# Writing the one-hots of a graph kernel's two gather stages on GpSimd, with an eight-part row ring in the first

## The reference

```python
q, k, v = h @ Wq + bq, h @ Wk + bk, h @ Wv + bv     # layer 2, per node; 8 heads of 16
e = edge_attr @ We                                  # per edge
alpha = sum(q[dst] * (k[src] + e)) / 4              # per edge and head
a = exp(alpha - segment_max(alpha, dst)[dst])
out = segment_sum(a / segment_sum(a, dst)[dst] * (v[src] + e), dst)
...
x_src, x_dst, x_edge = ...                          # layer 4, per edge, of h[src] and h[dst]
gates = softmax(concat(x_src, x_dst, x_edge) @ W_gate + b_gate)
out = segment_sum(gates[0] * x_src + gates[1] * x_dst + gates[2] * x_edge, dst)
```

## Time and profile before

| | |
|---|---|
| median of 3 runs | 7088.67 us (7060.04 to 7090.18) |
| span of the profiled execution | 7080.9 us |
| keys-and-values stage, first gather to last score | 2370.6 to 3815.0, 1444.4 us |
| gate stage, first gather to last addition | 5607.2 to 7030.2, 1423.0 us |
| DVE work in one-hots, gate stage | 144.3 us (208 of 694 ns) |

### The profile page before, as it was taken

One profiled execution on the slowest core, in us unless ns is written; L12 is line 12 of the kernel. 1 busy time (PEld: TensorE's weight loads), 2 busy tenths in 40 slices (PEclk: granted clock), 3 DMA queues, 4 the chain that ended last, 5 costly groups with the idle time before them and its releaser, 6 DMA issues.

```text
span 7080.9 us, 98147 instructions
## 1 busy us (share of the span) xinstructions
PE 4162.5 (59%) x25513; PEld 3308.9 (47%) x25514; DVE 2977.6 (42%) x8318; ACT 1295.5 (18%) x3253; POOL 2894.8 (41%) x2784
## 2 busy tenths in 40 slices
PE   1112000599898455555563664798899666666664
PEld 1001000366565455555553563465565666556654
DVE  3438201411313344444446677212312555555556
ACT  0001000000100211111111664200200322322222
POOL 6778777000000265555553565000000255555555
PEclk6555555799899777777776996899999755655555
DMA  9713000366463455555552451464364222222222
GB/s 361 267 61 135 6 0 0 103 198 192 141 195 118 111 160 158 154 150 156 155 162 89 125 148 30 137 197 138 131 196 145 64 78 78 78 78 79 79 78 69
DMA packets 447985, 885.48 MB, mean 125 GB/s; under 512 B 91722, under 2 KB 278572, under 8 KB 441502
## 3 DMA queue, kind: packets, MB, share of 16 engines
q1 hardware_dynamic: 333406, 608.36, 27.1%
q0 software_dynamic: 106912, 224.30, 11.9%
q10 hardware_dynamic: 7584, 51.91, 2.0%
HBM read 728.93 MB, written 155.35 MB: 125 GB/s over the span
## 4 chain that ended last, share of the span: by engine, by line
PE 33%; DVE 20%; issue 19%; another core or an unknown queue 15%; DVEq 6%; DMA 2%; ACT 2%; ACTq 1%; SPq 0%; POOL 0%; POOLq 0%
PE ps L836 23%; DVE work L1603 3%; PE ps L992 2%; DVE work L624 2%; PE ps L415 1%; DVE work L368 1%; DMA hw<-d_keys 1%; DVE work L1202 1%; DVEq L342 1%; PE ps L1184 1%; DVE hw L438 1%; PE ps L843 1%; PE ps L1182 1%; DMA work<-attr_dram 1%
## 5 line engine op out<-in xcount | busy, mean ns | idle before, releaser
L361 POOL DMA_INDIRECT work<-tab_kv,src_col x832 | 814.1, 978 | 1758.7 <-DMA tab_kv<-hw 1142.1
L361 POOL DMA_INDIRECT work<-tab_gate,src_col x832 | 795.5, 956 | 1795.5 <-DMA tab_gate<-logits 1183.3
L484 POOL DMA_INDIRECT d_adj<-logits,address x782 | 848.1, 1085 | 276.6 <-issue 238.8
L836 PE MATMUL ps<-hw 128*128 128x384 bf16 x5096 | 863.4, 330 | 50.4 <-DVE hw L815 37.1
L836 PE MATMUL ps<-hw,work 128*128 128x384 bf16 x5096 | 845.1, 326 | 0.0
L415 PE MATMUL ps<-work 128*128 128x136 f32 (+1 forms) x3328 | 655.0, 360 | 131.6 <-DVE acc L438 86.4
L836 PEld LDWEIGHTS ps<-hw 128*128 128x128 bf16 x5096 | 502.1, 99 | 383.1 <-issue 53.7
L415 PEld LDWEIGHTS ps<-work 128*128 128x128 f32 x3328 | 599.8, 265 | 165.4 <-issue 165.4
L875 DVE TENSOR_TENSOR work<-work,ps 128x128 f32 (+1 forms) x208 | 59.9, 288 | 1410.0 <-ACT work L867 1409.2
L836 PEld LDWEIGHTS ps<-hw,work 128*128 128x128 bf16 x5096 | 498.8, 98 | 317.7
L1168 PE MATMUL ps<-ident,work 128*128 128x128 f32 x832 | 177.1, 350 | 656.8 <-ACT work L1158 285.2
(11 more groups left out here) (389 smaller groups left out, 6581.4 us busy)
## 6 DMA issues: line engine op xcount, KB each, us to landing
hw<-d_adj SPq DMA_DIRECT2D x104, 800.0 KB, 4.3
work<-d_adj SPq DMA_DIRECT2D x104, 800.0 KB, 4.4
d_adj<-acc SPq DMA_DIRECT2D x52, 1568.0 KB
hw<-d_adj SPq DMA_DIRECT2D x104, 768.0 KB, 4.2
work<-d_adj SPq DMA_DIRECT2D x104, 768.0 KB, 4.3
work<-attr_dram SPq DMA_DIRECT2D x832, 64.0 KB
d_value<-work SPq DMA_DIRECT2D x208, 256.0 KB
work<-d_value SPq DMA_DIRECT2D x208, 256.0 KB, 2.7
```

Of the source, the lines that this page charges most:

```text
L361: pool.indirect_dma_start(rows[:, r * U + u, 0:width], None, table, bass.IndirectOffsetOnAxis(sources[:, at:at + 1], 0)).then_inc(rows_in[ ...
L484: pool.indirect_dma_start(d_adj, bass.IndirectOffsetOnAxis(address[:, tile:tile + 1], 0), counts[:, tile:tile + 1], None).then_inc(adj_out ...
L836: last = nc.tensor.matmul(at, adj_half[2 * s + hf][:, k, :], xs[:, b, :], start=b == 0, stop=b == BLOCKS - 1)
```

## The change

The one-hots of the two gather stages are written by POOL: behind each gather it puts one 128x128 compare (`tensor_scalar`) for the same step. In the keys-and-values stage the ring of gathered rows gets eight parts: four in `rows`, four in the space of `acc`. Since `acc` is in use until the scores are done, the load of `resets` moves behind the last score on SP. Some semaphores are merged (`x_and_h`, `relu_ready`, `x_biased`, and three of the beta step), and `edge_loop` takes the number of parts.

```diff
-        def gathers(pool, k, table, width, sources, free):
+        def gathers(pool, k, table, width, sources, free, hot_free):
             for n in range(GATHER_TURNS[k] * PARTS):
                 r = n % PARTS
                 if n >= PARTS:
                     free(n - PARTS)
                 for u in range(U):
                     at = n * U + u
                     pool.indirect_dma_start(rows[:, r * U + u, 0:width], None, table,
                                             bass.IndirectOffsetOnAxis(sources[:, at:at + 1], 0)).then_inc(rows_in[r], 16)
+                    if u == 0 and n >= PARTS:
+                        hot_free(n - PARTS)
+                    ins = pool.tensor_scalar(hot[:, r * U + u, :], iota[:], rel_col[:, at:at + 1], None, ALU.is_equal)
+                ins.then_inc(sem("hot_ready"), 1)
...
+        def kv_rows(r):
+            return (near_rows if r < PARTS else far_rows)[:, r % PARTS * U:(r % PARTS + 1) * U, :]
         def att_pool(pool):
             pool.wait_ge(sem("table_out"), KV_TABLE)
-            gathers(pool, ATT_PASS, tab_kv, KV, src_col, lambda n: pool.wait_ge(sem("kv_done"), n + 1))
+            for n in range(ALL_PARTS):
+                r = n % FAR
+                if n >= FAR:
+                    pool.wait_ge(sem("kv_done"), n - FAR + 1)
+                for u in range(U):
+                    at = n * U + u
+                    pool.indirect_dma_start(kv_rows(r)[:, u, :], None, tab_kv,
+                                            bass.IndirectOffsetOnAxis(src_col[:, at:at + 1], 0)).then_inc(far_in[r], 16)
+                    if u == 0 and n >= PARTS:
+                        pool.wait_ge(sem("att_turned"), n - PARTS + 1)
+                    ins = pool.tensor_scalar(hot[:, n % PARTS * U + u, :], iota[:], rel_col[:, at:at + 1], None, ALU.is_equal)
+                ins.then_inc(sem("hot_ready"), 1)
...
-            edge_loop(dve, [(0, step_hot()), (2, scores)])
+            edge_loop(dve, [(2, scores)], FAR_TURNS, FAR)
...
-            gathers(pool, GATE_PASS, tab_gate, GATE_ROW, src_col, lambda n: pool.wait_ge(sem("gate_msg"), n + 1))
+            gathers(pool, GATE_PASS, tab_gate, GATE_ROW, src_col, lambda n: pool.wait_ge(sem("gate_msg"), n + 1),
+                    lambda n: pool.wait_ge(sem("win_done"), gate_sums.done0 + U * (n + 1)))
...
-            edge_loop(dve, [(2, logits), (3, message), (2, gates), (0, step_hot(hot_free)), (4, gate_sums.step_add(dve))])
+            edge_loop(dve, [(2, logits), (3, message), (2, gates), (4, gate_sums.step_add(dve))])
...
-            max_sp(sp)
             att_sp(sp)
+            sp.wait_ge(sem("kv_done"), ALL_PARTS)
+            max_sp(sp)
             sums_sp(sp)
```

More of the change, by code:

```diff
@@ L23 @@
 ALL_PARTS = TURNS * PARTS
+FAR = 8
+FAR_TURNS = ALL_PARTS // FAR
+assert FAR_TURNS * FAR == ALL_PARTS and FAR == 2 * PARTS
 PAIRS = -(-TILES // 2)
@@ L80, in wait, with edge_loop @@
         engine.wait_ge(sem, value)
-def edge_loop(engine, stages, turns=TURNS):
-    for r in range(PARTS):
+def edge_loop(engine, stages, turns=TURNS, parts=PARTS):
+    for r in range(parts):
         for lag, step in stages:
             if r >= lag:
-                step((r - lag) // PARTS, (r - lag) % PARTS)
+                step((r - lag) // parts, (r - lag) % parts)
     with engine.Fori(1, turns) as i:
-        for r in range(PARTS):
+        for r in range(parts):
             for lag, step in stages:
-                back = (r - lag) // PARTS
-                step(i + back if back else i, (r - lag) % PARTS)
+                back = (r - lag) // parts
+                step(i + back if back else i, (r - lag) % parts)
     for late in range(max(lag for lag, _ in stages)):
@@ L97, in edge_loop @@
             if late < lag:
-                step(turns + (late - lag) // PARTS, (late - lag) % PARTS)
+                step(turns + (late - lag) // parts, (late - lag) % parts)
 def pair_loop(engine, count, step):
@@ L223, in program @@
         rows = part(rows_flat, 0, (TURN, GATE_ROW))
+        near_rows, far_rows = part(rows_flat, 0, (TURN, KV)), part(acc_flat, 0, (TURN, KV))
         hot = part(hot_flat, 0, (TURN, P))
@@ L323, in program @@
         rows_in = [sem(f"rows_in{r}") for r in range(PARTS)]
+        far_in = rows_in + [sem(f"far_in{r}") for r in range(FAR - PARTS)]
         attr_in = [sem(f"attr_in{r}") for r in range(PARTS)]
@@ L345, in registers @@
             return values
[L350 removed]
+        GATHER_TURNS = (FAR_TURNS, TURNS)
         TURN0 = [sum(GATHER_TURNS[:k]) for k in range(len(GATHER_TURNS))]
[L353 removed]
+        def gathers(pool, k, table, width, sources, free, hot_free):
             for n in range(GATHER_TURNS[k] * PARTS):
@@ L1190, in scores @@
             def scores(i, r):
-                n = i * PARTS + r
+                n = i * FAR + r
                 e = banks(2 + 2 * (r % RING2)).rearrange("p (u f) -> p u f", u=U)
                 q = banks(3 + 2 * (r % RING2)).rearrange("p (u f) -> p u f", u=U)
-                key = rows[:, r * U:(r + 1) * U, 0:D]
+                key, its_value = kv_rows(r)[:, :, 0:D], kv_rows(r)[:, :, D:KV]
                 values = value[:, r % RING2 * U:(r % RING2 + 1) * U, :]
                 dve.wait_ge(sem("eq_done"), n + 1)
-                dve.wait_ge(rows_in[r], 16 * U * (ATT_TURN0 + i + 1))
-                wait(dve, value_out[r % RING2], 16 * (i * (PARTS // RING2) + r // RING2))
+                dve.wait_ge(far_in[r], 16 * U * (i + 1))
+                wait(dve, value_out[r % RING2], 16 * (i * (FAR // RING2) + r // RING2))
                 nc.vector.tensor_tensor(key, e, key, ALU.add).then_inc(sem("key_step"), 1)
-                nc.vector.tensor_tensor(values, e, rows[:, r * U:(r + 1) * U, D:KV], ALU.add)
+                nc.vector.tensor_tensor(values, e, its_value, ALU.add)
                 dve.wait_ge(sem("key_step"), 2 * n + 1)
@@ L1430, in beta_act @@
         def beta_act(act):
-            act.wait_ge(sem("beta_in"), 1)
+            act.wait_ge(sem("beta_dve"), 1)
             nc.scalar.activation(stat[:, 1, :], stat[:, 0, :], ACT.Exp, scale=-1.0).then_inc(sem("beta_exp"), 1)
@@ L1467, in att_end_dve @@
             chain.after(nc.vector.reciprocal(stat[:, 2, :], stat[:, 1, :]))
-            dve.sem_inc(sem("beta_ready"), 1)
+            dve.sem_inc(sem("beta_dve"), 1)
             with chain.loop(GROUPS, 1) as g:
@@ L1507, in mix_act @@
         def mix_act(act):
-            act.wait_ge(sem("beta_ready"), 1)
+            act.wait_ge(sem("beta_dve"), 2)
             with act.Fori(0, GROUPS) as g:
@@ L1747, in _ @@
             sp.wait_ge(sem("reset_out"), 16)
+            att_sp(sp)
+            sp.wait_ge(sem("kv_done"), ALL_PARTS)
             max_sp(sp)
-            att_sp(sp)
             sums_sp(sp)
@@ L2030, in kv_ready @@
                 dve.sem_inc(sem("kv_ready"), 1)
-                nc.vector.tensor_tensor(group(x, g), group(x, g), group(h, g), ALU.add).then_inc(sem("x_and_h"), 1)
+                nc.vector.tensor_tensor(group(x, g), group(x, g), group(h, g), ALU.add).then_inc(sem("x_added"), 1)
             p_qkv.dve(dve, behind=kv_ready)
-            dve.wait_ge(sem("x_and_h"), GROUPS)
+            dve.wait_ge(sem("x_added"), GROUPS)
             att_dve(dve)
@@ L2054, in relu @@
             def relu(g):
-                nc.vector.tensor_scalar(group(t, g), group(t, g), 0.0, None, ALU.max).then_inc(sem("relu_ready"), 1)
+                nc.vector.tensor_scalar(group(t, g), group(t, g), 0.0, None, ALU.max).then_inc(sem("x_added"), 1)
             p_sage1.dve(dve, behind=relu)
-            dve.wait_ge(sem("relu_ready"), GROUPS)
+            dve.wait_ge(sem("x_added"), 2 * GROUPS)
             dve.sem_inc(sem("self2_ready"), GROUPS)
@@ L2060, in _ @@
             p_self2.dve(dve, behind=lambda g: nc.vector.tensor_tensor(
-                group(x, g), group(x, g), bias("L2_bn2", GROUP), ALU.add).then_inc(sem("x_biased"), 1))
-            dve.wait_ge(sem("x_biased"), GROUPS)
+                group(x, g), group(x, g), bias("L2_bn2", GROUP), ALU.add).then_inc(sem("x_added"), 1))
+            dve.wait_ge(sem("x_added"), 3 * GROUPS)
             dve.sem_inc(sem("dense_open"), 1)
```

9 lines of the change are left out of this document (2 added, 7 removed).

## The result

The changed kernel takes 7857.56 us (median of 4 runs, 7800.25 to 7863.54) against 7089.43 us (7060.04 to 7124.37): a ratio of 1.1055, 95% interval 1.1007 to 1.1103. I had forecast 7235 us, and a range up to 7560. The direction was right, the size was not.

The account below looks back on a forecast made before the run. No engine was over 59% busy; POOL's waits, read as PE's counts arriving late behind close gathers, bounded the two stages. 7080.9 - 146 + 46 + 247 = 7228 us profiled, 7235 us median; range 6990 to 7560 us.

Parts of the forecast that it names:

- The compare's price: Both gather stages: each POOL compare adds 0.30 us to the 1.25 us gather pitch, taken from an affine select.
- a pitch nearer 1.9 us: Sign of a wrong prediction: POOL's step of gather and compare near 1.9 us instead of the forecast 1.55 us.
- 1664 c - 352 us: Whole kernel: the change's total effect, with c the cost of one POOL compare; nothing at c = 0.21.
- Rival 3: Both stages: compare costs 0.5 to 0.6 us because POOL switches between descriptors and elements; 7570 to 7735 us; chance 0.10.
- Keys-and-values stage: POOL sets the pace at 6.20 us a part, start hole of 45 us gone: 1298 us against 1444, -146 us.
- The resets: End of keys-and-values stage: the load moved behind the last score takes 48 us and delays the first scan; +46 us.
- Gate stage: POOL and PE wait for each other once a part: 7.98 us a part against 6.79, +247 us.
- The circle: Gate stage: POOL's last compare, PE's turn and sums, then POOL's next one-hot; 3.03 us, POOL standing 1.8 us a part.
- rival 4: POOL's compares and DVE's messages with two SBUF operands hold each other up: +115 us, 7350 us; chance 0.08.
- rival 2: Keys-and-values stage: PE's counts still arrive late while gathers follow each other, and POOL waits: 7565 us; chance 0.13.
- Rival 5: Gate stage: PE's clock rises to 2.4 GHz, shortening the mutual wait to 6.4 us a part: 6935 us; chance 0.03.
- Rivals 1 and 6: Compare mostly fits the gap between gathers, 6903 us at 0.1 us, chance 0.20; or costs near 0.21 us, terms cancel, 0.06.

Follow-up runs that it names:

- spaced: Kernel before plus a useless one-element POOL compare behind the first three gathers of each part, both stages: 6239.74 us against 5916.44, ratio 1.055.
- const_compare: Changed kernel with POOL comparing with a constant, not the targets' column, and one 128x512 compare a part in the gate stage: 6727.0 us in one run.
- ring8_onedma: Changed kernel with DVE writing all one-hots and the reset load as one DMA: 5902.04 us against 5911.07 for the kernel before, ratio 0.998.
- sums_first: Changed kernel with PE doing sums(n-3) before turn(n) in the gate stage: 6935.11 us; that stage 1614.9 us against 1957.4.
- gate_only: Kernel before with only the gate stage's half of the change, POOL writing the gate's one-hots: 6758.86 us against 5917.88, ratio 1.142.
- att_only: Changed kernel with DVE writing the gate's one-hots again, so only the keys-and-values half: 6449.96 us, ratio 1.090 to the kernel before.
- the ring of eight: Changed kernel with DVE writing all one-hots and a one-DMA reset load, on both chip kinds: 7100.28 us against 7108.95, 5902.04 against 5911.07.

## Why the prediction was wrong

**The compare's price is the step that failed.** I took 0.30 us from the affine select as the nearest row. Measured is 0.62 us added to a step: 0.31 that a compare of one element costs between two gathers (spaced), and as much again that goes with the 128 elements, at 2.5 ns each (const_compare). It is what I had written down as a sign of being wrong, a pitch nearer 1.9 us. The select is no row for a compare: of the same shape, it takes half the time; why, no run shows. The other row that I named, the product of 128x512, would have warned: divided by four it gives 0.29, but that spreads the fixed part of one instruction over four; with the 0.21 us that spaced measured as fixed, 128 elements of it come to 0.45 us, an estimate. My own account said 1664 c - 352 us; with c = 0.62 it gives +680 us, or 7769 in the median. That is 534 of the 622 us by which I was short. Rival 3 (0.5 to 0.6 us, 7570 to 7735 us) had nearly the right size, but not by its reason, POOL's change of kind 1664 times: that can be no more than the 0.31 us of the smallest compare, and only 0.10 of these lie outside the compare's own record. I had given it 0.10.

**Keys-and-values stage.** The mechanism held: POOL sets the pace, four steps a part. Forecast -146 us, measured +117; 832 x 0.317 = 264 us lie between, all of it the compare. The 45 us hole at the start is gone: all of POOL's waits for scores are 9.1 us, where one alone was 42.7.

**The resets.** Forecast +46, measured +58.5. I took 48 us for the load, below the 59 that stood in the earlier trace rows, for the other traffic at that time; it took 59.9 us with far less beside it. Its form is what made it so long, as ring8_onedma shows: sixteen DMAs of 8 partitions take three times as long as one over 128. My 51 us had eight DMA engines busy all the time at the rate of the earlier trace rows; how many engines each DMA used was not looked at.

**Gate stage.** The circle was right in every member, 3.02 us against 3.03, and sums_first shows that it makes the wait. Forecast +247 with c = 0.30; with c = 0.62 the same formula gives 3.03 + 3.75 + 2.48 = 9.26 us a part, +514. Measured is 9.35 and +534. The last 20 us are rival 4, in small. By the trace of the changed kernel, 118 of the stage's 832 compares took over 0.66 us, each of them beside a message of DVE, and 119 gathers beside the last message took 1.14 to 1.16 us and not 1.03; that is 10 and 15 us in all. I had priced 115. Compares with no message beside them took 0.64 us at most, here and in sums_first. So did all 832 of the keys-and-values stage, where DVE's instructions with two inputs read one of them from PSUM; the messages read both from SBUF. That this is the reason is an inference from these rows; no run took the messages away. The Trainium skill, "SBUF — State Buffer", section "SBUF: two separate sides", has whichever of the two starts first hold the shared ports for its whole instruction, with the other fully blocked. The trace does not agree: the compare of 0.84 us in the stretch above ends at 6612.37, so it lies wholly within four messages that take 1.16 us (6611.36 to 6612.52), and four took 1.13 us before without a compare beside them; one behind the other they would need 1.13 + 0.63 = 1.76 us.

**Late counts** (rival 2). They did not stay: in the changed kernel all 208 starts of ACT follow PE's last transpose within 0.12 us. At steps of 1.87 us they are not there. What I had read from the earlier trace rows was true of that chip. Against a chip of the second kind, where the stages were left alone (gate_only, att_only), it is 342 us in the one stage (1444.4 against 1102.5) and 296 us in the other (1423 against 1126.8). There the counts are not late, POOL's gathers alone set the pace of the kernel before, and each of the change's halves costs more. That is also why the same change is worth 1.10 on one kind and, by its halves, about 1.23 on the other.

**The other rivals.** Rival 5 did not come: PE's clock in the gate stage is 0.55, against 0.56 before. Rivals 1 and 6 needed a compare of 0.21 us or less. Two of my sums were off by a little: c from 0.25 to 0.36 gives 7153 to 7336 us and not 7120 to 7340, and the terms of rival 5 give 6.6 us a part and some 6950 us, not 6.4 and 6935.

**What stays open.** What makes one kind of chip post PE's counts late. Whether spacing the gathers would cure it: the run made for that met a chip of the other kind. The difference of the kinds ahead of the keys-and-values stage: of some 1170 us between them, 527 lie there (2370.6 against 1843.7), and no run was made for it; POOL has 782 other indirect DMAs in that stretch. The 52 us ahead of the first gather: on one chip of the second kind there is no such difference (1840.1 to 1843.7 us in four profiles, with and without the ring), on the first kind the start lay at 2406 to 2444 us in four profiles of changed kernels and at 2370.6 in the one of before, while the kernel before itself varies by over 100 us there (7044.74 to 7148.84). I can't say which it is.

## What to carry to other kernels

Price an instruction that an engine has not run in this kernel from a row of the same operation, or treat its cost as open up to the largest plausible row: a fixed part and a part per element must be known apart, and a loop that repeats it 1664 times makes each 0.1 us of doubt 166 us. An engine whose row of work sets a stage's pace gets nothing more to do; DVE, which gave the work away, was 45 to 53% busy in these stages and won nothing. Where two engines wait for each other once a turn, write down the circle and look for a member that can be taken out by order alone: one line gave back 342 us.

## What the runs showed of the hardware

- GpSimd's compare of a row with a constant: 0.21 us for 1 element, 0.54 for 128, 1.50 for 512, so 0.21 us and 2.5 ns an element. Between two gathers it adds 0.31, 0.64 and 1.6 us, 0.1 more than its own time. With a scalar of each partition, 128 elements are 0.63 us busy but add no more, 0.62 us.
- A gather behind an elementwise instruction is 1.03 us busy, one behind another gather 0.95 (spaced).
- A compare of GpSimd beside DVE instructions that read two operands from SBUF took 0.81 to 0.92 us in sums_first and not 0.63; four such DVE instructions took 1.16 us and not 1.13.
- Sixteen DMAs that each broadcast one row of 26,624 bytes to 8 partitions take 59.9 us; one DMA of the same bytes over 128 partitions 19.2 us.
- Two kinds of times were met for the kernel before, 7100 and 5915 us, each on several chips. Of the difference 527 us lie ahead of the first gather of keys and values, 342 and 296 us in the two gather stages, and nothing between these (1792.2 and 1793.0 us, at a clock of 0.90 on both). Stages whose pace POOL or the circle sets took 1562 to 1566 and 1957 to 1958 us on both kinds. The mean granted clock of the ring of eight was 0.740 on the one and 0.795 on the other; no run shows whether that is cause or consequence.
